# Last layer's edge pass: both ends' parts meet with channels on partitions, destination rows become TensorE weights, scan resets spread by a product

## Chip, core and metric

The kernel runs on one core of a Trainium2 chip. The metric is the device time of one execution in microseconds. A core has five engines that run side by side and meet at semaphores: PE (matmul; PEld is its weight load), DVE (elementwise, scans), ACT (activation functions), POOL and SP. SP here only issues DMAs. SBUF is the on-chip memory, PSUM the banks that PE writes.

## What is computed

Four graph layers over 6250 nodes of 128 channels and 106250 edges, sorted by destination; between them a layer norm with the residual. The change touches only the last one:

```python
f_src = (feat @ W_src.T + b_src).reshape(n, HEADS, OUT_FEATS)
f_dst = (feat @ W_dst.T + b_dst).reshape(n, HEADS, OUT_FEATS)
f_v = (feat @ W_v.T + b_v).reshape(n, HEADS, OUT_FEATS)
a = f_src[src] + f_dst[dst]
e = jnp.where(a >= 0, a, NEG_SLOPE * a)
sa = _edge_softmax(e, dst, n)          # per channel, over the edges of a destination
m = f_v[src] * sa
rst = jax.ops.segment_sum(m, dst, num_segments=n)
```

The softmax is per channel: for each destination and channel the maximum over its edges, the exponentials of what lies below it, their sum.

## The kernel before

Each layer is a pass over the edges (`edges0` to `edges3`) and a pass over the nodes (`after0` to `after3`). An edge pass goes over items: an item is a chunk of 128 edges together with a tile of 128 nodes that holds their destinations. Four items are a group, and there are 220 groups. `pipeline` runs the groups in steps: in step v every stage with lag k works on group v - k, and within a step each engine takes its stages in the order of the list that `ps.run` gets. That list is the whole schedule; a step is as long as its slowest ring of waits. Ten steps are one turn of a hardware loop.

In `edges3`, for one group:

- `gather` (lag 0): SP waits for `s_others` and `s_gap` of two groups ago, then loads `near` (L926; two buffers), a row of 516 floats spread to all 128 partitions, which says for each edge which node of the tile it belongs to. POOL gathers the rows of the edges' sources (L808, four indirect DMAs), 256 floats an edge: the source part and the value part. Every fifth step SP also loads indices (L792).
- `load_resets` (lag 2): SP waits for the backward scan of two groups before (`s_top`), then spreads a row of `reset_d` to all partitions (L1359): 0 within a destination, hugely negative where the next one begins.
- `turn` (lag 0, ACT): L1371 and L1377 make the selector `sel_t` (node on partitions, edge along the row) out of `near`; `not_first` (L1384) and `from_first` (L1391, gap) follow. `s_gap` releases the next load of `near`.
- `both_ends` (lag 1, PE): `sel_t` as weights times the nodes' destination parts (L1400, `side(...)` is the destination part of a tile in `acc`, its place read from a register), plus a product with `ident` that adds the source parts (L1402). The result has edges on partitions.
- `take` (lag 2, ACT L1406) copies it, `leaky` (lag 2, DVE L1411) applies the slope. `by_channel` (lag 2, PE L1419) transposes, so that channels are on partitions.
- `forward` (lag 3, DVE L1430): a scan along the edges, state = max(state + reset, logit), in place in PSUM. `backward` (lag 3, DVE L1438): the same from the right. Now each edge holds its destination's maximum, in `top`.
- `below_top` (lag 4, PE): `top` times -1 (L1484) brings the maximum back to edges on partitions, a product with `ident` adds the logit (L1486). `exps` (lag 4, ACT L1490).
- `message` (lag 5): exponentials times values, L1496, items 0 and 1 on POOL, 2 and 3 on DVE. `sums_a` and `sums_b` (lag 5, PE L869) multiply with the selector `sel` (made by ACT, L844 and L852) and so add up per node; DVE adds four items to `acc` (lag 6, L893) behind a rescaling (L1475).

PE's order in a step is `below_top`, `both_ends`, `by_channel`, `factors`, `sums_a`, `sums_b`; DVE's is `leaky`, `scaled`, three adds, `message`, the last add, `forward`, `backward`; SP's is near, indices, resets.

Of the kernel before, what the change touches and what calls it, by code (L numbers as in the profile page):

```python
# [15 lines left out]
P = 128  # L16
N_NODES = 6250
N_EDGES = 106250
D = 128
# [22 lines left out]
LOW = -3.0e38  # L42
# [108 lines left out]
def build(nc, a):  # L151
    PE, V, A, G, SP = nc.tensor, nc.vector, nc.scalar, nc.gpsimd, nc.sync
# [3 lines left out]
    def dram(name, shape, dt=F32):  # L156
        return nc.dram_tensor(name, shape, dt).ap()
# [3 lines left out]
    reset_d = dram("reset_d", [ITEMS_PAD // GROUP, GROUP * P])  # L161
# [17 lines left out]
    def sb(ctx, name, shape, dt=F32):  # L179
        return ctx.enter_context(nc.sbuf_tensor(name, shape, dt))  # L180
# [12 lines left out]
    ident = sb(root, "ident", [P, P])  # L193
# [21 lines left out]
    def tables(ctx, closing, loaded_x, loaded_qkv, made_ident, cleared_x):  # L215
# [102 lines left out]
        m = pe.did(m)  # L318
# [38 lines left out]
        reset = sb(ctx, "reset", [P, ITEM_TILES, P])  # L357
# [582 lines left out]
    def quad(b, width=P):  # L940

        return bank[b][:, 0:GROUP * width].rearrange("p (i d) -> p i d", i=GROUP)
# [376 lines left out]
    def edges3():  # L1319
# [3 lines left out]

        with Phase(nc, "e3") as ctx:
            ps = EdgePass(ctx, fsv_t, 2 * D, W3, sels=2, turns=1)
            EDGES = GROUP * P
            resets = ps.sb("resets", [P, 2, EDGES + 1])
# [7 lines left out]
            s_resets = [ps.sem(f"resets{u}") for u in range(2)]  # L1335
            s_a, s_taken, s_l, s_turned, s_run, s_top, s_d, s_exp, s_msg_g, s_msg_v = (
                ps.sem(n) for n in ("a", "taken", "l", "turned", "run", "top", "d", "exp", "msg_g", "msg_v"))
# [6 lines left out]
            V.memset(resets[:, :, EDGES:], 0.0).then_inc(start, 1)  # L1344
# [48 lines left out]
            def both_ends(g):  # L1393
                tiles = ps.tiles(g, PE_ENGINE)
                ps.have_rows(PE, g)
                PE.wait_ge(by_node.s_t, g.upto(0))
                if g.old(2):
                    PE.wait_ge(s_l, g.upto(-2))
                for i in range(GROUP):
                    PE.matmul(bank[B_A[g.r2]][:, i * P:(i + 1) * P], by_node.sel_t[:, g.r2, i, :],  # L1400
                              side(ds(tiles[i], 1)).rearrange("p a d -> p (a d)"), start=(i == 0), stop=False)
                PE.matmul(quad(B_A[g.r2]), ident[:], ps.row(g)[:, :, 0:D], start=False, stop=True).then_inc(s_a, 1)  # L1402

            def take(g):
                A.wait_ge(s_a, g.upto(0))
                A.activation(ps.row(g)[:, :, 0:D], quad(B_A[g.r2]), ACT.Copy).then_inc(s_taken, 1)  # L1406

            def leaky(g):

                V.wait_ge(s_taken, g.upto(0))  # L1410
                V.scalar_tensor_tensor(out=ps.row(g)[:, :, 0:D], in0=quad(B_A[g.r2]), scalar=0.2,  # L1411
                                       in1=ps.row(g)[:, :, 0:D], op0=ALU.mult, op1=ALU.max).then_inc(s_l, 1)
# [12 lines left out]
            def forward(g):  # L1425
                V.wait_ge(s_turned, g.upto(0))
                V.wait_ge(s_resets[g.r2], (g.turn(2) + 1) * 16)
                if g.old(1):
                    V.wait_ge(s_top, g.upto(-1))
                V.tensor_tensor_scan(bank[B_L[g.r2]], resets[:, g.r2, 0:EDGES], bank[B_L[g.r2]],  # L1430
                                     top_before(g), ALU.add, ALU.max).then_inc(s_run, 1)

            def backward(g):
                V.wait_ge(s_run, g.upto(0))
                if g.old(SPAN):
                    V.wait_ge(s_d, g.upto(-SPAN))
                    V.wait_ge(s_rise, g.upto(1 - SPAN))
                V.tensor_tensor_scan(top[:, g.at(SPAN), ::-1], resets[:, g.r2, EDGES:0:-1],  # L1438
                                     bank[B_L[g.r2]][:, ::-1], LOW, ALU.add, ALU.max).then_inc(s_top, 1)
# [39 lines left out]
            def below_top(g):  # L1479
                PE.wait_ge(s_top, g.upto(0))  # L1480
                if g.old(1):
                    PE.wait_ge(s_exp, g.upto(-1))
                for i in range(GROUP):
                    PE.matmul(bank[B_D][:, i * P:(i + 1) * P], top[:, g.at(SPAN), i * P:(i + 1) * P], minus[:],  # L1484
                              start=(i == 0), stop=False)
                PE.matmul(quad(B_D), ident[:], ps.row(g)[:, :, 0:D], start=False, stop=True).then_inc(s_d, 1)  # L1486

            def exps(g):
                A.wait_ge(s_d, g.upto(0))
                A.activation(ps.row(g)[:, :, 0:D], quad(B_D), ACT.Exp).then_inc(s_exp, 1)  # L1490

            def message(engine, s_msg, items):
                def stage(g):
                    engine.wait_ge(s_exp, g.upto(0))
                    values = ps.row(g)[:, items, D:2 * D]
                    engine.tensor_tensor(values, values, ps.row(g)[:, items, 0:D], ALU.mult).then_inc(s_msg, 1)  # L1496
                return stage

            def sums_a(g):
                PE.wait_ge(s_msg_g, g.upto(0))  # L1500
                PE.wait_ge(ps.s_sel, g.upto(0))
                ps.scatter(g, lambda i: [(0, ps.row(g)[:, i, :])], (0, 1))

            def sums_b(g):
                PE.wait_ge(s_msg_v, g.upto(0))
                ps.scatter(g, lambda i: [(0, ps.row(g)[:, i, :])], (2, 3))

            ps.run([(0, gather), (2, load_resets), (5, message(G, s_msg_g, slice(0, 2))),
                    (4, below_top), (1, both_ends), (2, by_channel), (5, factors), (5, sums_a), (5, sums_b),
# [3 lines left out]
                    (5, message(V, s_msg_v, slice(2, 4))), (6, ps.add(3)), (3, forward), (3, backward)])  # L1513
# [59 lines left out]
```

## Time and profile before

| | |
|---|---|
| median of 3 runs | 5292.35 us (5288.9 to 5292.99) |
| profiled execution | 5294.54 us, span 5292.8 us |
| busy over the whole span | PE 3755.0 us (71%), DVE 3648.3 (69%), ACT 2912.2 (55%), POOL 3691.8 (70%) |
| last layer's edge pass | about 3848 to 5190 us of the span |
| SP's DMAs in it | near 258.0 KB, resets 256.0 KB a group; indices 10.0 KB every fifth |

Busy time is the time in which an engine has an instruction; for PE the ends are modelled, and instructions overlap. PEclk is the clock that PE was granted, as a share of 2.4 GHz; its other level is 1.2 GHz (0.50). The DMA share is the mean busy share of the core's 16 DMA engines. In the last edge pass the pattern repeats every 6 us or so, so one step on the time line and one table over many steps tell nearly everything. In rows with "issue" as releaser, the engine waited for nothing that the profile shows.

### The profile page before, as it was taken

To read this page: it belongs to the slowest core of one execution; us is meant where nothing else is said; L and a number is where in the kernel's file an instruction comes from. 1 tells how busy PE (TensorE), PEld (TensorE's weight loads), DVE (VectorE), ACT (ScalarE), POOL (GpSimd) and SP (SyncE) were. 2 spreads that over 40 slices of the span, in tenths; PEclk is the share of its full clock that TensorE was granted. 3 is DMA by queue.
4 is the path that set the end of the run, shared out by engine and by line. 5 is a ranking of instruction groups with operands and counts; after the bars stand their busy time and mean duration, and the time that the engine had idled before them with its cause. 6 is when DMAs were issued, how large, how long until landed. Compare 5 with 4: busy or idle time off the path is not lost. (4 is left out here: it accounts for less than half of the span.)

```text
span 5292.8 us, 95054 instructions
## 1 busy us (share of the span) xinstructions
PE 3755.0 (71%) x19843; PEld 3029.5 (57%) x19844; DVE 3648.3 (69%) x8656; ACT 2912.2 (55%) x7558; POOL 3691.8 (70%) x3835
## 2 busy tenths in 40 slices
PE   5444544441666566666678888888779999999992
PEld 4444444441555555555466666666657777777771
DVE  5666666667644444445577777777668989989997
ACT  2444444443522222223566666666469989999993
POOL 4777777773777777774377777777067777777772
PEclk8777877875777777777688898998989999999996
DMA  7444444442433333331111111111156666666661
GB/s 193 143 155 159 153 151 152 152 152 75 114 79 77 76 78 78 79 78 42 48 55 56 55 55 55 55 56 55 51 155 177 177 174 176 176 177 176 176 178 39
DMA packets 394829, 596.70 MB, mean 113 GB/s; under 512 B 115000, under 2 KB 224718, under 8 KB 394352
## 3 DMA queue, kind: packets, MB, share of 16 engines
q0 software_dynamic: 141696, 349.47, 23.6%
q1 hardware_dynamic: 252176, 245.81, 15.8%
q8 instruction: 32, 0.52, 0.0%
q10 hardware_dynamic: 864, 0.39, 0.0%
q14 instruction: 61, 0.50, 0.0%
HBM read 563.33 MB, written 30.30 MB: 112 GB/s over the span
## 5 line engine op out<-in xcount | busy, mean ns | idle before, releaser
L893 DVE TENSOR_TENSOR acc<-acc,banks 128x256 f32 (+1 forms) x3520 | 1360.8, 387 | 756.5 <-PE banks L869 486.2
L808 POOL DMA_INDIRECT e_rows<-kv_t,e_index x800 | 786.6, 983 | 243.7 <-issue 240.9
L808 POOL DMA_INDIRECT e_rows<-x_t,e_index x800 | 781.0, 976 | 248.6 <-issue 243.2
L808 POOL DMA_INDIRECT e_rows<-up_t,e_index x800 | 774.9, 969 | 243.8 <-issue 238.3
L808 POOL DMA_INDIRECT e_rows<-fsv_t,e_index x800 | 779.1, 974 | 227.0 <-issue 211.2
L869 PE MATMUL banks<-e_rows,e_sel 128*128 128x256 f32 x3520 | 904.1, 403 | 6.3 <-ACT e_rows L1095 3.8
L844 ACT ACTIVATE e_away<-node_iota,local 128x128 f32<-128x128 f32 x2640 | 840.5, 389 | 8.4 <-issue 0.9
L869 PE MATMUL banks<-e_msg,e_sel 128*128 128x137 f32 (+1 forms) x3520 | 760.8, 365 | 9.9 <-DVE acc L893 4.5
L869 PEld LDWEIGHTS banks<-e_rows,e_sel 128*128 128x128 f32 x3520 | 681.7, 204 | 99.3 <-issue 6.8
L970 PE MATMUL banks<-acc,e_sel_t 128*128 x1760 | 312.3, 333 | 586.2 <-DVE e_sel_t L937 571.8
L1095 ACT ACTIVATE e_rows<-banks,e_rows 128x128 f32<-128x128 f32 x880 | 250.7, 370 | 799.5 <-PE banks L1086 384.1
L869 PEld LDWEIGHTS banks<-e_msg,e_sel 128*128 128x128 f32 x3520 | 625.5, 219 | 60.5 <-DVE acc L893 4.9
L970 PEld LDWEIGHTS banks<-acc,e_sel_t 128*128 128x128 f32 x1760 | 272.0, 236 | 621.8 <-issue 620.9
L1086 PE MATMUL banks<-e_w,e_attr 65*128 65x128 f32 x1760 | 289.3, 317 | 406.4 <-DMA e_attr<-in_attr_rows 406.0
L1086 PEld LDWEIGHTS banks<-e_w,e_attr 65*128 65x128 f32 x1760 | 275.6, 228 | 439.9 <-issue 387.0
L852 ACT ACTIVATE e_sel<-e_away,ones_col 128x512 f32<-128x512 f32 x660 | 473.4, 717 | 21.3
L999 ACT ACTIVATE e_msg<-e_clip 128x32 f32<-128x32 f32 x220 | 51.1, 232 | 658.6 <-DVE e_clip L995 657.6
L937 DVE TENSOR_SCALAR e_sel_t<-e_near,node_step 128x512 f32<-128x512 f32 x220 | 113.1, 514 | 319.0 <-DMA e_near<-near_d 318.9
L1400 PEld LDWEIGHTS banks<-acc,e_sel_t 128*128 128x128 f32 x1760 | 232.5, 193 | 129.2 <-issue 129.2
L1221 PE MATMUL banks<-e_emb,e_w 16*128 16x256 f32 x440 | 164.7, 456 | 180.9 <-DMA e_emb<-emb_d 161.4
L1430 DVE TENSOR_TENSOR_SCAN banks<-e_resets,e_top,banks 128x512 f32<-128x512 f32 x220 | 281.9, 1282 | 0.0
L1438 DVE TENSOR_TENSOR_SCAN e_top<-e_resets,banks 128x512 f32<-128x512 f32 x220 | 268.6, 1221 | 10.8 <-DVE banks L1430 3.9
(202 smaller groups left out, 6973.4 us busy)
## 6 DMA issues: line engine op xcount, KB each, us to landing
e_near<-near_d SPq DMA_DIRECT2D x440, 258.0 KB, 5.2
e_resets<-reset_d SPq DMA_DIRECT2D x220, 256.0 KB
e_attr<-in_attr_rows SPq DMA_DIRECT2D x880, 32.0 KB
e_rows<-kv_t,e_index POOLq DMA_INDIRECT x800
e_rows<-x_t,e_index POOLq DMA_INDIRECT x800
e_rows<-up_t,e_index POOLq DMA_INDIRECT x800
e_rows<-fsv_t,e_index POOLq DMA_INDIRECT x800
kv_t<-proj_kv SPq DMA_DIRECT2D x12, 512.0 KB, 5.3
```

The lines of the kernel that those rows point to most:

```text
L808: G.indirect_dma_start(out=self.rows[:, u, i, 0:self.width], out_offset=None, in_=self.table, in_offset=bass.IndirectOffsetOnAxis(ap=index ...
L844: m = A.activation(away[:, i, :], node_iota[:], ACT.Abs, bias=local[:, ds(g.n * GROUP + i, 1)], scale=-1.0)
L852: A.activation(self.place_of_sel(g), away[:], ACT.Relu, bias=ones_col[:], scale=-1.0).then_inc(self.s_sel, 1)
L869: m = PE.matmul(bank[n_bank][:, col + at:col + at + rows.shape[1]], self.place_of_sel(g)[:, i, :], rows, start=True, stop=True)
L893: V.tensor_tensor(to, to, bank[n_bank][:, col:col + self.sums].unsqueeze(1), ALU.add).then_inc(self.s_added[i], 1)
L970: m = PE.matmul(bank[B_Q[g.r2]][:, i * P:(i + 1) * P], by_node.sel_t[:, g.r2, i, :], side(ds(tiles[i], 1)).rearrange("p a d -> p (a d)"), ...
L1086: m = PE.matmul(bank[B_H[g.r2]][:, i * P:(i + 1) * P], attr[:, g.at(SPAN), i, :], w1[:], start=True, stop=True)
L1095: m = A.activation(ps.row(g)[:, i, D + 1:], bank[B_H[g.r2]][:, i * P:(i + 1) * P], ACT.Relu, scale=ps.row(g)[:, i, 0:1])
L1221: PE.matmul(hidden_bank(g, 0), w0[:], emb[:, g.at(SPAN), :], start=True, stop=True).then_inc(s_h1, 1)
L1400: PE.matmul(bank[B_A[g.r2]][:, i * P:(i + 1) * P], by_node.sel_t[:, g.r2, i, :], side(ds(tiles[i], 1)).rearrange("p a d -> p (a d)"), star ...
L1430: V.tensor_tensor_scan(bank[B_L[g.r2]], resets[:, g.r2, 0:EDGES], bank[B_L[g.r2]], top_before(g), ALU.add, ALU.max).then_inc(s_run, 1)
L1438: V.tensor_tensor_scan(top[:, g.at(SPAN), ::-1], resets[:, g.r2, EDGES:0:-1], bank[B_L[g.r2]][:, ::-1], LOW, ALU.add, ALU.max).then_inc(s_ ...
```

## The change

Both parts of the logit now meet with channels on partitions. `both_ends` transposes the gathered source parts into the bank and adds a product whose weights are the destination parts of the tile and whose moving side is `sel_t`. The weights are no longer read from `acc` under a register; SP copies each of the group's four tiles into a buffer `far` first (`load_far`). `take` and `leaky` write `logit`, five groups deep, and `by_channel` goes. The resets are loaded as one BF16 row, and PE spreads them to the 128 partitions of a PSUM bank by a product with a row of ones (`spread_resets`, lag 3). The scans read the resets there; the forward scan writes `top` in SBUF, the backward one runs in place over its 511 other elements. `below_top` transposes the logits back and adds the negated tops, with two banks instead of one. POOL multiplies one item of the message instead of two, DVE three. `load_resets` moves from lag 2 to lag 1 and waits for `s_r` of two groups before.

```diff
-            resets = ps.sb("resets", [P, 2, EDGES + 1])
+            far = ps.sb("far", [P, 2, GROUP, P])
+            logit = ps.sb("logit", [P, SPAN, EDGES])
+            resets = ps.sb("resets", [1, 2, EDGES], BF16)
+            ones_row = ps.sb("ones_row", [1, P], BF16)
...
-            B_A, B_L, B_D, B_F = (2, 3), (4, 5), 6, 7
+            B_A, B_D, B_R, B_F = (2, 3), (4, 5), 6, 7
...
+            def load_far(g):
+
+                tiles = ps.tiles(g, SP_ENGINE)
+                if g.old(2):
+                    SP.wait_ge(s_a, g.upto(-2))
+                for i in range(GROUP):
+                    SP.dma_start(far[:, g.r2, i, :], side(ds(tiles[i], 1)).rearrange("p a d -> p (a d)")
+                                 ).then_inc(s_far[g.r2], 16)
+
             def load_resets(g):
                 if g.old(2):
-                    SP.wait_ge(s_top, g.upto(-2))
-                SP.dma_start(resets[:, g.r2, 0:EDGES], reset_d[ds(g.n, 1), :].to_broadcast([P, EDGES])
-                             ).then_inc(s_resets[g.r2], 16)
+                    SP.wait_ge(s_r, g.upto(-2))
+                SP.dma_start(resets[:, g.r2, :], reset_d[ds(g.n, 1), :]).then_inc(s_resets[g.r2], 16)
...
             def both_ends(g):
-                tiles = ps.tiles(g, PE_ENGINE)
                 ps.have_rows(PE, g)
                 PE.wait_ge(by_node.s_t, g.upto(0))
+                PE.wait_ge(s_far[g.r2], (g.turn(2) + 1) * 64)
                 if g.old(2):
                     PE.wait_ge(s_l, g.upto(-2))
                 for i in range(GROUP):
-                    PE.matmul(bank[B_A[g.r2]][:, i * P:(i + 1) * P], by_node.sel_t[:, g.r2, i, :],
-                              side(ds(tiles[i], 1)).rearrange("p a d -> p (a d)"), start=(i == 0), stop=False)
-                PE.matmul(quad(B_A[g.r2]), ident[:], ps.row(g)[:, :, 0:D], start=False, stop=True).then_inc(s_a, 1)
+                    PE.matmul(bank[B_A[g.r2]][:, i * P:(i + 1) * P], ps.row(g)[:, i, 0:D], ident[:],
+                              start=(i == 0), stop=False, is_transpose=True)
+                for i in range(GROUP):
+                    m = PE.matmul(bank[B_A[g.r2]][:, i * P:(i + 1) * P], far[:, g.r2, i, :],
+                                  by_node.sel_t[:, g.r2, i, :], start=False, stop=(i == GROUP - 1))
+                m.then_inc(s_a, 1)
...
-            def by_channel(g):
-                PE.wait_ge(s_l, g.upto(0))
-                if g.old(2):
-                    PE.wait_ge(s_top, g.upto(-2))
-                for i in range(GROUP):
-                    m = PE.transpose(bank[B_L[g.r2]][:, i * P:(i + 1) * P], ps.row(g)[:, i, 0:D], ident[:])
-                m.then_inc(s_turned, 1)
+            def spread_resets(g):
+                PE.wait_ge(s_resets[g.r2], (g.turn(2) + 1) * 16)
+                if g.old(1):
+                    PE.wait_ge(s_top, g.upto(-1))
+                PE.matmul(bank[B_R], ones_row[:], resets[:, g.r2, :], start=True, stop=True).then_inc(s_r, 1)
...
-                V.tensor_tensor_scan(bank[B_L[g.r2]], resets[:, g.r2, 0:EDGES], bank[B_L[g.r2]],
-                                     top_before(g), ALU.add, ALU.max).then_inc(s_run, 1)
...
+                V.tensor_tensor_scan(top[:, g.at(SPAN), :], bank[B_R], logit[:, g.at(SPAN), :],
+                                     top_before(g), ALU.add, ALU.max).then_inc(s_run, 1)
+
+            def backward(g):
+
+                V.wait_ge(s_run, g.upto(0))
+                back = top[:, g.at(SPAN), EDGES - 2::-1]
+                V.tensor_tensor_scan(back, bank[B_R][:, EDGES - 1:0:-1], back, top[:, g.at(SPAN), EDGES - 1:EDGES],
+                                     ALU.add, ALU.max).then_inc(s_top, 1)
...
                 for i in range(GROUP):
-                    PE.matmul(bank[B_D][:, i * P:(i + 1) * P], top[:, g.at(SPAN), i * P:(i + 1) * P], minus[:],
-                              start=(i == 0), stop=False)
-                PE.matmul(quad(B_D), ident[:], ps.row(g)[:, :, 0:D], start=False, stop=True).then_inc(s_d, 1)
+                    PE.matmul(bank[B_D[g.r2]][:, i * P:(i + 1) * P], logit[:, g.at(SPAN), i * P:(i + 1) * P], ident[:],
+                              start=(i == 0), stop=False, is_transpose=True)
+                for i in range(GROUP):
+                    m = PE.matmul(bank[B_D[g.r2]][:, i * P:(i + 1) * P], top[:, g.at(SPAN), i * P:(i + 1) * P], minus[:],
+                                  start=False, stop=(i == GROUP - 1))
+                m.then_inc(s_d, 1)
...
-            ps.run([(0, gather), (2, load_resets), (5, message(G, s_msg_g, slice(0, 2))),
-                    (4, below_top), (1, both_ends), (2, by_channel), (5, factors), (5, sums_a), (5, sums_b),
+            ps.run([(0, gather), (0, load_far), (1, load_resets), (5, message(G, s_msg_g, slice(0, 1))),
+                    (4, below_top), (3, spread_resets), (1, both_ends), (5, factors), (5, sums_a), (5, sums_b),
...
-                    (5, message(V, s_msg_v, slice(2, 4))), (6, ps.add(3)), (3, forward), (3, backward)])
+                    (5, message(V, s_msg_v, slice(1, 4))), (6, ps.add(3)), (3, forward), (3, backward)])
```

## Rows read from the trace of the kernel before

**Rows 1.** Windows, all engines: busy us (instructions) by engine, PEclk, DMA share, GB/s

```profile
2904.60:2908.00 3.40, 0.10 (x1) 0.11 (x2) 1.90 (x6) 0.56 (x1) 2.49 (x4) 1.00 0.20 51
...
866.00:877.00 11.00, 6.29 (x48) 5.69 (x48) 9.45 (x27) 6.74 (x20) 8.56 (x9) 1.00 0.35 105
4200.00:4800.00 600.00, 594.65 (x3311) 450.38 (x3310) 541.28 (x905) 546.99 (x1405) 463.80 (x502) 1.00 0.63 176
```

**Rows 2.** Waits from 4200 to 4800: us in total, times, longest

```profile
ACT e_apart L1371 <- DMA e_near<-near_d: 38.7, 82, 1.7
PEld banks L1484 <- DVE e_top L1438: 26.3, 84, 0.9
...
DVE e_rows L1411 <- ACT e_rows L1406: 5.8, 14, 1.2
```

**Rows 3.** Time line of SP and ACT from 4507: start, length in us

```profile
4507.06 0.33 SPq L926 DMA_DIRECT2D e_near<-near_d  x1
4510.65 0.72 ACT L1371 ACTIVATE e_apart<-e_near,e_minus_node 128x512 f32<-128x512 f32 x1 [0.35 <-DMA e_near<-near_d]
...
4512.36 0.39 ACT L1391 ACTIVATE e_gap<-node_iota,e_near 128x128 f32<-128x128 f32 x1
4512.97 0.34 SPq L926 DMA_DIRECT2D e_near<-near_d  x1
4513.54 0.51 SPq L792 DMA_DIRECT2D e_index<-src  x1
4516.38 0.72 ACT L1371 ACTIVATE e_apart<-e_near,e_minus_node 128x512 f32<-128x512 f32 x1
```

**Rows 4.** Line L926 from 4200 to 4800: duration, first and last start

```profile
L926 SPq DMA_DIRECT2D e_near<-near_d x101: 332/333/338, 4200.7 to 4799.2; - x101
```

**Rows 5.** Time line of DVE, a step in which it isn't kept waiting

```profile
4221.68 0.67 DVE L1411 SCALAR_TENSOR_TENSOR e_rows<-banks,e_rows 128x512 f32<-128x512 f32 x1
...
4224.38 0.42 DVE L1496 TENSOR_TENSOR e_rows<-e_rows 128x256 f32<-128x256 f32 x1
4224.72 0.41 DVE L893 TENSOR_TENSOR acc<-acc,banks 128x256 f32 x1
4225.05 1.28 DVE L1430 TENSOR_TENSOR_SCAN banks<-e_resets,e_top,banks 128x512 f32<-128x512 f32 x1
4226.36 1.22 DVE L1438 TENSOR_TENSOR_SCAN e_top<-e_resets,banks 128x512 f32<-128x512 f32 x1
4227.50 0.67 DVE L1411 SCALAR_TENSOR_TENSOR e_rows<-banks,e_rows 128x512 f32<-128x512 f32 x1
```

**Rows 6.** Time line of PE, a step from its beginning

```profile
4503.81 1.09 PE L1484 MATMUL banks<-e_minus,e_top 128*128 128x128 f32 x8
4504.74 1.02 PE L1486 MATMUL banks<-e_rows,ident 128*128 128x512 f32 x2
4505.60 1.05 PE L1400 MATMUL banks<-acc,e_sel_t 128*128 x8
4506.49 1.02 PE L1402 MATMUL banks<-e_rows,ident 128*128 128x512 f32 x2
4507.35 0.60 PE L1419 MATMUL banks<-ident,e_rows 128*128 128x128 f32 x4
4507.79 0.27 PE L1464 MATMUL banks<-ident,e_at_first 128*128 128x128 f32 x1
```

**Rows 7.** Groups of DVE instructions, first layer's pass, 500 to 1100: busy, mean ns

```profile
L1004 DVE TENSOR_TENSOR e_msg<-e_rows,e_msg 128x512 f32<-128x512 f32 x118 | 80.9, 685 | 0.0
```

**Rows 8.** Time line of SP in the second layer's pass: DMAs of 32 KB with dynamic addresses

```profile
1699.70 6.55 SPq L1078 DMA_DIRECT2D e_attr<-in_attr_rows  x9
```

**Rows 9.** SP's own waits from 4200 to 4800

```profile
SPq L1359 <- DVE e_top L1438: 250.0, 100, 3.1
```

**Rows 10.** DMA queue of SP, 4200 to 4800 and 5225 to 5290: packets, MB, share of 16 engines

```profile
q1 hardware_dynamic: 31762, 52.99, 30.9%
...
q1 hardware_dynamic: 6444, 3.20, 17.1%
```

More of the change, by code:

```diff
@@ L160, in build @@
     item_rows = dram("item_rows", [2, ITEMS_PAD], I32)
-    reset_d = dram("reset_d", [ITEMS_PAD // GROUP, GROUP * P])
+    reset_d = dram("reset_d", [ITEMS_PAD // GROUP, GROUP * P], BF16)
     rhat_d = dram("rhat_d", [P, ITEMS_PAD, 3])
@@ L356, in tables @@
         near = sb(ctx, "near", [P, ITEM_TILES, P + 1])
-        reset = sb(ctx, "reset", [P, ITEM_TILES, P])
+        reset = sb(ctx, "reset", [P, ITEM_TILES, P], BF16)
         yield V, 2.2
@@ L1334, in edges3 @@
             apart = ps.sb("apart", [P, GROUP, P])
-            s_resets = [ps.sem(f"resets{u}") for u in range(2)]
-            s_a, s_taken, s_l, s_turned, s_run, s_top, s_d, s_exp, s_msg_g, s_msg_v = (
-                ps.sem(n) for n in ("a", "taken", "l", "turned", "run", "top", "d", "exp", "msg_g", "msg_v"))
+            s_resets, s_far = ([ps.sem(f"{n}{u}") for u in range(2)] for n in ("resets", "far"))
+            s_a, s_taken, s_l, s_r, s_run, s_top, s_d, s_exp, s_msg_g, s_msg_v = (
+                ps.sem(n) for n in ("a", "taken", "l", "r", "run", "top", "d", "exp", "msg_g", "msg_v"))
             s_apart, s_gap, s_rise, s_shrink, s_first, s_f, s_others, s_scaled, start = (
                 ps.sem(n) for n in ("apart", "gap", "rise", "shrink", "first", "f", "others", "scaled", "start"))
-            B_A, B_L, B_D, B_F = (2, 3), (4, 5), 6, 7
+            B_A, B_D, B_R, B_F = (2, 3), (4, 5), 6, 7
             by_node = ByNode(ps, s_a, 2)
@@ L1343, in edges3 @@
             V.memset(top[:, SPAN - 1, :], LOW).then_inc(start, 1)
-            V.memset(resets[:, :, EDGES:], 0.0).then_inc(start, 1)
+            V.memset(ones_row[:], 1.0).then_inc(start, 1)
             V.tensor_scalar(minus[:], ident[:], -1.0, None, ALU.mult).then_inc(start, 1)
@@ L1399, in both_ends @@
                 for i in range(GROUP):
[L1400 to L1402 removed]
+                    PE.matmul(bank[B_A[g.r2]][:, i * P:(i + 1) * P], ps.row(g)[:, i, 0:D], ident[:],
[4 more added lines that the diff above has]
+                m.then_inc(s_a, 1)
             def take(g):
                 A.wait_ge(s_a, g.upto(0))
[L1406 removed]
+                if g.old(SPAN):
+                    A.wait_ge(s_d, g.upto(-SPAN))
+                A.activation(logit[:, g.at(SPAN), :], bank[B_A[g.r2]], ACT.Copy).then_inc(s_taken, 1)
             def leaky(g):
                 V.wait_ge(s_taken, g.upto(0))
[L1411 to L1420 removed]
+                V.scalar_tensor_tensor(out=logit[:, g.at(SPAN), :], in0=bank[B_A[g.r2]], scalar=0.2,
+                                       in1=logit[:, g.at(SPAN), :], op0=ALU.mult, op1=ALU.max).then_inc(s_l, 1)
+            def spread_resets(g):
[3 more added lines that the diff above has]
+                PE.matmul(bank[B_R], ones_row[:], resets[:, g.r2, :], start=True, stop=True).then_inc(s_r, 1)
             def top_before(g):
@@ L1425, in forward @@
             def forward(g):
-                V.wait_ge(s_turned, g.upto(0))
-                V.wait_ge(s_resets[g.r2], (g.turn(2) + 1) * 16)
+                V.wait_ge(s_l, g.upto(0))
+                V.wait_ge(s_r, g.upto(0))
                 if g.old(1):
                     V.wait_ge(s_top, g.upto(-1))
-                V.tensor_tensor_scan(bank[B_L[g.r2]], resets[:, g.r2, 0:EDGES], bank[B_L[g.r2]],
+                if g.old(SPAN):
+                    V.wait_ge(s_d, g.upto(-SPAN))
+                    V.wait_ge(s_rise, g.upto(1 - SPAN))
+                V.tensor_tensor_scan(top[:, g.at(SPAN), :], bank[B_R], logit[:, g.at(SPAN), :],
                                      top_before(g), ALU.add, ALU.max).then_inc(s_run, 1)
```

15 lines of the change are left out of this document (5 added, 10 removed).

## Prediction

> **What bounds the kernel now.** I read the page first: nothing outside the last layer's edge pass is touched, so only its 220 steps count (a step is one group of four items). There PE looks like the bound: in 600 us of steady running it is busy for 594.65, at the full clock, against 541 for DVE, 547 for ACT and 464 for POOL [rows 1]. The change takes work off PE, so the question is whether that busy figure is a bound. A busy figure with modelled ends can't say; the waits can, and then the time line.
>
> The list of waits says that PE waits for DVE (PEld L1484 on the backward scan, 84 times in 101 steps, 26.3 us), DVE waits for ACT's copy 14 times (5.8 us), and ACT waits for the DMA of near 82 times (38.7 us of 600, the largest wait that isn't "issue" among those that end at another engine or a DMA) [rows 2]. So the chain of blame ends at a DMA, and the reader should see what that DMA itself waits for. On the time line near is issued at 4507.06, ACT's L1371 starts on it at 4510.65, L1391 starts at 4512.36 and lasts 0.39, and 0.22 later, at 4512.97, the next near goes out [rows 3]. That is a closed ring, because near has two buffers: load(g) waits for gap(g-2), which ACT makes one step before it needs near(g). Its length in this step is 3.59 (issue to start) + 1.71 + 0.39 + 0.22 = 5.91 us. Over the stretch 101 issues lie between 4200.7 and 4799.2, which is 598.5 / 100 = 5.985 us a step [rows 4]. With 2.32 us for the three fixed terms, the mean from issue to use is 5.985 - 2.32 = 3.66 us. The ring accounts for the whole step, and there is no PE in it.
>
> Two other chains lie just under it. DVE's step, where it isn't kept waiting, is 4227.50 - 4221.68 = 5.82 us [rows 5]. PE's step is 5.985 less the 0.26 us that PEld waits for the backward scan, about 5.7 [rows 2]. POOL and ACT have more room; ACT waits 0.4 us a step.
>
> **The change part by part.** My sum is made against the profiled execution, 5294.54 us with a span of 5292.8; the median of the runs is 5292.35, so 2.2 us are taken off at the end.
>
> *PE.* Removed: the two 512-column products with ident, 0.86 each (4504.74 to 4505.60, 4506.49 to 4507.35), and the by_channel transposes, 0.44 (4507.35 to 4507.79). Added: two sets of four transposes at 0.44 and the spread of the resets. The far products keep L1400's 0.89, the top products L1484's 0.93 [rows 6]. The spread is one pass over 512 columns in BF16; no row shows it. From below it is a single 128-column transpose, 0.11, from above a 512-column product in F32, 0.86; I take a quarter of that, 0.22, since L1402 takes two records for its 0.86 and each column of a transpose costs half of those again. Sum: -0.86 -0.86 -0.44 +0.88 +0.22 = -1.06 us a step, 233 us over 220 steps. I cost this saving at nothing: PE would stand idle for about 1.3 us instead of 0.3. Its step still begins at DVE's backward scan, and its sums still need ACT's selector of the same step.
>
> *DVE.* leaky keeps shape and operand kinds (PSUM and SBUF in, SBUF out). The forward scan now writes SBUF instead of PSUM. Backward already does, and takes 1.22 against 1.28 [rows 5]; so -0.06, bounds -0.06 and 0 (both scans now read the resets from PSUM and the data from SBUF, one PSUM operand as before; +0.06 each is the far end if the operand's place matters). The message goes from two items to three. 512 elements out of SBUF take 0.685 [rows 7], 256 take 0.42, so 128 more cost 0.133. Sum +0.07: DVE's floor becomes 5.82 + 0.07 = 5.89 us, bounds 5.82 and 6.01. This is the price that matters: whatever else the change frees, a step can't fall by more than 5.985 - 5.89 = 0.095 us, or 21 us in all.
>
> *POOL.* Its message loses one of two items. It isn't on the ring, so nothing is gained.
>
> *ACT.* The same instructions with the same shapes; take writes logit instead of rows. Zero. Two new waits (take on s_d of five steps ago) are long fulfilled.
>
> *SP and the DMA queues.* This is where the ring can be hurt. Per step the 256 KB broadcast of the resets goes, a row of 1 KB comes, and four SBUF-to-SBUF copies of 64 KB come with a register load, directly behind near. In the second layer's pass nine such DMAs with a dynamic address, with their register loads, take 6.55 us, 0.73 each [rows 8]; four are 2.9 us of SP. SP has them in the step's 5.985 us beside near, the resets and every fifth step the indices. What stands behind them is load_resets, which now waits for PE's spread instead of for DVE's backward scan: 1.37 + 0.22 + about 0.2 later than that scan's end. PE's step of 4503.81 [rows 6] has its successor near 4509.8, so the spread is done at about 4511.6, SP is through with the resets half a us later, 4512.1, and gap ends at 4512.75. So near isn't held up as long as DVE is no more than 0.6 us late. SP's present waits, 2.5 us a step for the scan, say that there is room [rows 9]. Price 0; if the cover is gone, each us of lateness goes into the ring in full.
>
> The load on the DMA engines: near and resets are 30.9% of the 16 engines, about 15.5% each. The 512-byte packets of the output (6444 of them, 17.1% of 16 engines over 65 us) cost 0.0276 us each [rows 10]; 512 of them a step are 14.1 us on 16 engines, 14.8% of 5.985. So far weighs what the resets weighed. It only moves: resets went out some 3 us before near, far goes out up to 3 us behind it. Near's landing of 3.66 us is the term that decides, and no row shows it with four DMAs behind. The nearest is 4512.97, with the index DMA 0.57 behind it: 3.41 to L1371, against 3.59 for the one before without [rows 3]. Bounds: 0.15 shorter (no resets ahead, gathers less backed up) and 0.3 longer (near shares the engines with its followers); ACT's longest single wait, 1.7 us, shows that landings do stretch. I take 0 for the mean.
>
> The Trainium skill speaks against the far copies: DMA: Bandwidth & Descriptors (Bandwidth) asks for DMAs of 1 MiB and gives 0.95 us for one of 64 KB. An estimate by that page would be 3.8 us of DMA time a step for the four (measured there for DMAs that another engine issues), against 0.88 by the packets of this trace. What it would mean here is rival 5.
>
> **Sum.** The ring stays at 5.985. It has some scatter, which DVE today makes good between long landings; with DVE's floor raised that costs a little, and with the resets gone from ahead of near a little comes back. I put the net at -0.02 us a step: 220 x -0.02 = -4 us, 5290.3 on the profiled execution and 5288 against the median.
>
> **Rivals.**
> 1. *The followers delay near.* For it: one queue, four DMAs behind it in every step, gathers in between. Against it: near's packets are first in their queue and the engines' load is equal. 0.1 to 0.3 us a step, 22 to 66 us; middle 5325. It decides from a landing of 3.72 on, since there is no slack in the ring: 0.05 x 220 = 11 us. This is the case slower than before.
> 2. *PE is the bound after all*, or the landing gets shorter by 0.1 or more. Both end at the same wall, DVE's 5.89: -0.095 x 220 = -21, 5272. For it: 99% busy, and the broadcast ahead of near is gone. Against it: the ring closes without PE, and PE waits for DVE in most steps.
> 3. *DVE's new floor binds.* If the scans dislike the resets in PSUM (+0.06 each), the floor is 6.01 and the step with it: +0.03 x 220, 5298; with ordinary lateness on top, 5303.
> 4. *PE's clock.* PE gets idle time. In this trace the clock stays at 2.4 GHz with PE only 57% busy in 866 to 877, and falls to 1.2 GHz behind the stretch from 2904.6, in which it did 0.1 us of work in 3.4 [rows 1]. With 1.3 us idle in 6 I expect the first. If it fell in one step of five, the 1.6 us from the scan's end to the spread would double there, use up the 0.6 of slack and delay near by 1.0: 0.2 a step, +44, 5332. By TensorE: Matmul & The Clock Gate (Part 1: The HAM clock gate) of the Trainium skill the throttled clock is the default and activity lifts it, so that less work is a risk; the row at 57% speaks against it here.
> 5. *Small transfers are dear.* If a far packet cost what one of the resets does (15.5% for 128), 512 would be 62%, the DMA load 0.63 - 0.155 + 0.62 = 1.10 and the step 5.985 x 1.10 = 6.56: +127, 5415. The output's packets speak against it. It is how the page above would come true.
> 6. *The change doesn't do what it says*: the old copies and products stay. The diff removes them; under 1%.
>
> **How the numbers follow.** Forecast (landing within -0.09 and +0.05 of now) 44%, 5280 to 5300. Rival 1 20%, rival 2 25%, rival 3 5%, rival 4 with other lateness of SP 4%, rivals 5 and 6 2%. Two runs of this kernel can be told apart from about 0.2%, 10.6 us. Of the forecast a few hundredths fall beyond either edge; faster 0.28, same 0.44, slower 0.28. The range goes from 5270, just under DVE's wall, to 5330, which takes in most of rival 1; about 2 in 10 stay outside.
>
> **What would show it.** In the changed kernel's trace: step time by the issues of near; issue of near to L1371's successor (3.66 now); ACT's wait for near (0.4 us a step now; gone if DVE's wall is reached); DVE's unhindered step, 5.89; scans at 1.22 both; the message on DVE at 0.55; PE about 1.3 us idle a step, its clock at 1.00; DMA share still near 0.63. I am wrong if near's landing moves by more than 0.1 us, if SP issues near later than 0.22 us behind gap, or if DVE's step isn't 5.89.

## The result, and the profile after

The changed kernel takes 5305.98 us (median of 8 runs, 5301.47 to 5308.46), the kernel before 5289.11 us (8 runs, 5285.12 to 5295.06) on the same chip. The ratio is 1.003, with a 95% interval from 1.0019 to 1.004: slower by 17 us. The profiled execution has a span of 5306.7 us. The predicted 5288 lay on the other side of no change; the time is inside the range of 5270 to 5330.

The loss lies in the last layer's pass. In the two profiled executions, whose spans are 5292.8 and 5306.7 us, the time from the first to the last issue of near grows by 16.2 us; this pass starts 2.0 us earlier, and the part behind the last near changes by 0.3. A step of the pass is read from the issues of near over a long stretch, 4000 to 5100 us (columns: instructions; shortest, median and longest ns; first and last start). Before:

```profile
L926 SPq DMA_DIRECT2D e_near<-near_d x184: 332/333/338, 4005.0 to 5098.1; - x184
```

and after:

```profile
L926 SPq DMA_DIRECT2D e_near<-near_d x182: 332/349/353, 4003.6 to 5099.0; - x182
```

That is 1093.1 / 183 = 5.973 us a step before and 1095.4 / 181 = 6.052 after. The difference, 0.079 us, times 220 steps is 17.4 us, as much as the medians differ by: the loss is in the length of the step.

The windows row of after, 4200 to 4800 us (busy us and instructions of PE, PEld, DVE, ACT, POOL; PEclk; DMA share; GB/s), stands against the last line of [rows 1]:

```profile
4200.00:4800.00 600.00, 530.40 (x3374) 427.99 (x3375) 549.35 (x894) 540.65 (x1388) 430.23 (x497) 1.00 0.63 174
```

PE lost 64 us of 595, the clock stayed at 2.4 GHz (1.00), and the DMA share is the 0.63 of before. The only engine that is busier is DVE, though it did fewer steps. The waits of after in the same stretch say where PE's gain went, and what became of the ring (us in total, times, longest):

```profile
PEld banks L1503 <- DVE e_top L1457: 84.0, 85, 1.3
PE banks L1503 <- DVE e_top L1457: 57.4, 91, 0.9
ACT e_apart L1386 <- DMA e_near<-near_d: 47.1, 95, 1.1
...
DVE e_logit L1430 <- ACT e_logit L1426: 0.4, 2, 0.2
...
SPq L1375 <- PE banks L1437: 138.2, 97, 2.0
SPq L925 <- ACT e_gap L1406: 14.3, 37, 1.0
```

PE's saving became waiting for DVE's backward scan: the wait of PE's weight loads is 84.0 us instead of 26.3 [rows 2]. ACT still waits for near, and a bit longer. The lines that decide are DVE's and the last one: DVE waits for ACT only twice, 0.4 us (before 14 times, 5.8 us [rows 2]), and SP holds near back for gap in only 37 of 99 steps. In the kernel before it did so in every one:

```profile
SPq L925 <- ACT e_gap L1391: 225.0, 101, 3.5
```

So the ring of near, closed in each step before, is mostly open after: the near for the next step is free to go when SP gets to it. What is closed instead is DVE's own chain. Its time line in after, from one forward scan to the next (start, length, both us):

```profile
4299.89 1.27 DVE L1450 TENSOR_TENSOR_SCAN e_top<-banks,e_top,e_logit 128x512 f32<-128x512 f32 x1
4301.19 1.28 DVE L1457 TENSOR_TENSOR_SCAN e_top<-banks,e_top 128x511 f32<-128x511 f32 x1
4302.39 0.66 DVE L1430 SCALAR_TENSOR_TENSOR e_logit<-banks,e_logit 128x512 f32<-128x512 f32 x1
4302.98 0.47 DVE L1494 SCALAR_TENSOR_TENSOR acc<-banks,e_others,acc 128x256 f32 x1
4303.55 0.98 DVE L893 TENSOR_TENSOR acc<-acc,banks 128x256 f32 x2
4304.75 0.42 DVE L893 TENSOR_TENSOR acc<-acc,banks 128x256 f32 x1 [0.21 <-DVE acc L893]
4305.09 0.55 DVE L1519 TENSOR_TENSOR e_rows<-e_rows 128x384 f32<-128x384 f32 x1
4305.55 0.41 DVE L893 TENSOR_TENSOR acc<-acc,banks 128x256 f32 x1
4305.89 1.27 DVE L1450 TENSOR_TENSOR_SCAN e_top<-banks,e_top,e_logit 128x512 f32<-128x512 f32 x1
...
4311.89 1.27 DVE L1450 TENSOR_TENSOR_SCAN e_top<-banks,e_top,e_logit 128x512 f32<-128x512 f32 x1
...
4317.89 1.27 DVE L1450 TENSOR_TENSOR_SCAN e_top<-banks,e_top,e_logit 128x512 f32<-128x512 f32 x1
```

The scan starts at 4299.89, 4305.89, 4311.89 and 4317.89: a step of exactly 6.00 us, again and again, with no wait for another engine. So regular a beat points to the engine that bounds; in the kernel before, whose ring goes through a DMA, the step varies more (the forward scan starts at 4242.49, 4248.60, 4254.41 and 4260.32: 6.11, 5.81 and 5.91 us). The difference is one of degree. Between 4000 and 5100 us, 144 of 182 steps of after lie within 0.03 us of the shortest; in the kernel before it is 86 of 184. So the kernel before, too, runs nearly half of its steps at DVE's own 5.82 us; the others are longer. In after some longer steps (such as 4347.90 to 4354.51) lift the mean to 6.05.

DVE's unhindered step was 5.82 [rows 5]; the prediction had 5.89 for after, and it is 6.00. Two lines of each kernel, from the groups of instructions of 4200 to 4800 (busy us, mean ns), hold most of the answer. Before:

```profile
L1430 DVE TENSOR_TENSOR_SCAN banks<-e_resets,e_top,banks 128x512 f32<-128x512 f32 x101 | 129.4, 1282 | 0.0
L1438 DVE TENSOR_TENSOR_SCAN e_top<-e_resets,banks 128x512 f32<-128x512 f32 x100 | 122.1, 1221 | 5.0 <-DVE banks L1430 1.9
```

After:

```profile
L1457 DVE TENSOR_TENSOR_SCAN e_top<-banks,e_top 128x511 f32<-128x511 f32 x100 | 128.0, 1280 | 3.5
L1450 DVE TENSOR_TENSOR_SCAN e_top<-banks,e_top,e_logit 128x512 f32<-128x512 f32 x99 | 126.2, 1275 | 0.0
...
L1519 DVE TENSOR_TENSOR e_rows<-e_rows 128x384 f32<-128x384 f32 x99 | 55.1, 556 | 0.0
```

The forward scan didn't get shorter (1.282 to 1.275), and the backward scan, costed at no change, got longer by 0.059 us. With the message's 0.134 that is 5.82 - 0.007 + 0.059 + 0.134 = 6.006.

### The profile page after: what moved, and what is told of

The parts are those of the page before. It is cut to its first block and busy times, and to the rows that moved or that the text cites. A ratio compares the mean times of both kernels' runs of the same rounds, so it can differ in the third digit from the quotient of the medians.

```text
span 5306.7 us, 96549 instructions
## 1 busy us (share of the span) xinstructions
PE 3639.6 (69%) x20063; PEld 3004.1 (57%) x20064; DVE 3680.0 (69%) x8656; ACT 2909.3 (55%) x7558; POOL 3627.0 (68%) x3835
## 5 line engine op out<-in xcount | busy, mean ns | idle before, releaser
L869 PE MATMUL banks<-e_rows,e_sel 128*128 128x256 f32 x3520 | 920.6, 408 | 22.9 <-issue 14.7
L970 PEld LDWEIGHTS banks<-acc,e_sel_t 128*128 128x128 f32 x1760 | 274.0, 237 | 617.4 <-issue 616.5
L1457 DVE TENSOR_TENSOR_SCAN e_top<-banks,e_top 128x511 f32<-128x511 f32 x220 | 281.7, 1280 | 7.8
L1450 DVE TENSOR_TENSOR_SCAN e_top<-banks,e_top,e_logit 128x512 f32<-128x512 f32 x220 | 280.5, 1275 | 0.3 <-issue 0.3
L1252 PEld LDWEIGHTS banks<-e_w,e_h 65*128 65x128 f32 x1760 | 259.6, 212 | 18.2 <-issue 3.8
```

Source lines behind the costliest of these rows:

```text
L869: m = PE.matmul(bank[n_bank][:, col + at:col + at + rows.shape[1]], self.place_of_sel(g)[:, i, :], rows, start=True, stop=True)
L970: m = PE.matmul(bank[B_Q[g.r2]][:, i * P:(i + 1) * P], by_node.sel_t[:, g.r2, i, :], side(ds(tiles[i], 1)).rearrange("p a d -> p (a d)"), ...
L1252: m = PE.matmul(bank[B_W[g.r2]][:, i * P:(i + 1) * P], h2[:, g.r2, i * P:(i + 1) * P], w2[:], start=True, stop=True)
L1450: V.tensor_tensor_scan(top[:, g.at(SPAN), :], bank[B_R], logit[:, g.at(SPAN), :], top_before(g), ALU.add, ALU.max).then_inc(s_run, 1)
L1457: V.tensor_tensor_scan(back, bank[B_R][:, EDGES - 1:0:-1], back, top[:, g.at(SPAN), EDGES - 1:EDGES], ALU.add, ALU.max).then_inc(s_top, 1)
```

## The experiments

Theory A: DVE's chain of 6.00 us binds, and is longer than the 5.82 of before by the third message item (0.13) and the backward scan (0.06). Rivals: near is held up behind SP's new order or by the far copies (rival 1 of the prediction); the resets in PSUM make the scans dear (the mechanism of rival 3). A chip's own median differs a little from the next one's, so each comparison below is with runs of the kernel before on the same chip. Steps are worked out as above, from the issues of near between 4000 and 5100 us.

**The message back at two items and two, in the changed kernel.**

```
-message(G, s_msg_g, slice(0, 1))    message(V, s_msg_v, slice(1, 4))
+message(G, s_msg_g, slice(0, 2))    message(V, s_msg_v, slice(2, 4))
```

(and the sums take items 0 and 1, then 2 and 3).

> The changed kernel with the message split as before: items 0 and 1 on POOL, 2 and 3 on DVE. Theory A (DVE's own chain of 6.00 us sets the changed kernel's step, since the message takes 0.134 us more and the scans read a PSUM operand): the chain falls to 5.87 us, the ring of near (2.32 + 3.59 = 5.91 us, and what SP adds) binds next, the step goes from 6.05 to about 5.95 us, the time from 5306 to about 5284 us. Theory B (SP's new work sets the step: four copies, and the wait for the spread ahead of near): DVE's part doesn't matter, 5306 us within 4.

5316.08 us against 5312.17 (ratio 1.0008, 0.9999 to 1.0017). The changed kernel itself was not run on this chip; against its ratios of 1.003 and 1.0034 on two others, most of the loss is gone. But the gain on the kernel before that theory A had expected isn't there. DVE's shortest steps fell to 5.87 us (4257.88 to 4263.75), and near's ring closed again: SP waited for gap in 89 of 99 steps. The expectation had taken near's landing from the first chip. Here the step is (5097.5 - 4002.2) / 180 = 6.085 us, and the time from the issue of near to the start of ACT's L1386 on it, taken for each near of the trace, has a mean of 3.72 us, against 3.62 in the kernel before on the first chip.

```profile
SPq L925 <- ACT e_gap L1406: 47.3, 89, 1.0
```

**The message at one item and three, in the kernel before**: the same edit the other way round.

> The kernel before with the message split of the changed one: item 0 on POOL, 1 to 3 on DVE, nothing else. Theory A: DVE's chain goes from 5.82 to 5.95 us, just under the ring's 5.97, so that DVE can't make good long landings any more: step 6.00 to 6.03 us, time 5289 + 220 x 0.04 = 5298 us (5295 to 5302). Theory B: nothing on SP changed, 5289 us.

```profile
4202.95 1.28 DVE L1430 TENSOR_TENSOR_SCAN banks<-e_resets,e_top,banks 128x512 f32<-128x512 f32 x1
...
4208.90 1.28 DVE L1430 TENSOR_TENSOR_SCAN banks<-e_resets,e_top,banks 128x512 f32<-128x512 f32 x1
```

5322.06 us (ratio 1.002, 1.001 to 1.0029): about 10 us slower, as theory A had it. DVE's shortest step is now 5.95 us. The third item on DVE (POOL has one less) costs time by itself, with none of the rest of the change there. It does so although the ring is closed in this kernel (SP waits for gap in 99 of 99 steps). That fits with the steps at DVE's own length counted above: with a longer one, DVE makes good less after a late landing. No run shows this reason by itself.

**Near with five buffers, in the kernel before.** This opens the ring and changes nothing else.

```
-by_node = ByNode(ps, s_a, 2)        g.old(2): SP.wait_ge(s_others, g.upto(-2))
+by_node = ByNode(ps, s_a, 5)        g.old(5): SP.wait_ge(s_others, g.upto(-5))
-by_node.near[:, g.r2, ...]          # in first() and turn()
+by_node.near[:, g.at(5), ...]
```

> The kernel before with five buffers for near instead of two, so that its load may go out three steps earlier. If the ring of near sets the step before (issue to use 3.66 us + 2.32 us of ACT and SP), it opens: ACT's wait for near (0.40 us a step) goes, the step falls to DVE's chain of 5.82 us with its loop end, about 5.87, and the time to 5289 - 220 x 0.11 = 5265 us. If PE or DVE set it already, 5289 us within 4.

5254.81 us against 5312.17 (ratio 0.9893, 0.9878 to 0.9908), 57 us faster (4 runs): the fastest kernel of this study. The expectation, made from the first chip, was 24 us. The step is (5095.2 - 4004.1) / 187 = 5.835 us; against the 5.973 of the kernel before on the first chip that would be 30 us, an estimate. The landings are longer on this chip, so there is more to win; there is no trace of the kernel before on it that would show its step. SP has no wait for gap left, and DVE's forward scans start at a beat of 5.82 us:

```profile
4298.35 1.28 DVE L1430 TENSOR_TENSOR_SCAN banks<-e_resets,e_top,banks 128x512 f32<-128x512 f32 x1
...
4304.17 1.28 DVE L1430 TENSOR_TENSOR_SCAN banks<-e_resets,e_top,banks 128x512 f32<-128x512 f32 x1
...
4309.98 1.28 DVE L1430 TENSOR_TENSOR_SCAN banks<-e_resets,e_top,banks 128x512 f32<-128x512 f32 x1
```

while the windows row has PE busy all the time:

```profile
4200.00:4800.00 600.00, 600.00 (x3396) 461.29 (x3394) 547.52 (x927) 564.81 (x1439) 472.21 (x515) 1.00 0.60 180
```

This confirms the reading of the kernel before: near's ring bound it and PE, at 594.65 of 600 [rows 1], did not; PE has done 2% more steps in the same 600 us without any of its work removed. That DVE is next, and not PE with its 600.00, is read from the waits: PE's weight loads wait for the backward scan 92 times in 4200 to 4800 us, and DVE waits 1.4 us in all for another engine (ACT). The change makes just that engine's step longer. The changed kernel with five buffers was not run, so what the change would be worth with the ring open is not shown.

**The resets broadcast into SBUF in BF16, in the changed kernel**, without the product that spreads them into PSUM. `load_resets` is back at lag 2 and waits for the backward scan, as in the kernel before.

```
-SP.dma_start(resets[:, g.r2, :], reset_d[ds(g.n, 1), :])                  # [1, 2, EDGES]
+SP.dma_start(resets[:, g.r2, :], reset_d[...].to_broadcast([P, EDGES]))   # [P, 2, EDGES]
-V.tensor_tensor_scan(top[...], bank[B_R], logit[...], ...)
+V.tensor_tensor_scan(top[...], resets[:, g.r2, :], logit[...], ...)
```

> The changed kernel with the resets spread by the DMA into SBUF again (in BF16, 128 KB a group), no product for them; the scans have no operand in PSUM. Theory A: both scans lose the PSUM read, 1.28 to 1.22 us each, DVE's chain falls from 6.00 to 5.88 us, the step to about 5.96 us, the time to 5306 - 220 x 0.09 = 5286 us. If the 0.06 us is not the operand's place (but, say, the reversed or in-place access), the scans stay at 1.28 and the time at 5306. Theory B (near held up by SP's wait for the spread): that wait goes too, 5290 us or less, but with the scans' length unchanged or not, ACT's wait for near falls.

```profile
L1455 DVE TENSOR_TENSOR_SCAN e_top<-e_resets,e_top 128x511 f32<-128x511 bf16 x96 | 123.6, 1288 | 3.4
L1448 DVE TENSOR_TENSOR_SCAN e_top<-e_resets,e_top,e_logit 128x512 f32<-128x512 bf16 x96 | 122.6, 1278 | 0.0
...
4200.00:4800.00 600.00, 489.30 (x3138) 409.06 (x3139) 536.63 (x857) 518.53 (x1332) 492.01 (x476) 0.99 0.71 188
```

5355.49 us (ratio 1.0079, 1.0065 to 1.0092). No operand of either scan is in PSUM, and they still take 1.28 us: the mechanism of rival 3 falls. (The resets are BF16 here, a second difference; in `before_ptr` below they are F32 in SBUF and the scans take 1.28 us as well.) The run is slower for another reason. The broadcast of 128 KB in every step raises the DMA share to 0.71, and the step is (5096.9 - 4004.6) / 173 = 6.314 us. SP waits for gap in 94 of 95 steps, so the ring binds, and 6.31 less the fixed 2.32 leaves 3.99 us from issue to use. The kernel before with the message at one and three, on the same chip, has a share of 0.63 and (5097.9 - 4002.4) / 180 - 2.32 = 3.77 us. Taken near by near from the traces the means are 3.96 and 3.74. So near lands later where more is moved beside it; how much of that is the load and how much the order in SP's queue, this run doesn't tell apart. Theory A's 5286 us did not come, since the scans did not get shorter and the load was not in its sum. Within this change, the spread by a product was the cheaper way: 1.0079 here against 1.003 and 1.0034 for the changed kernel on other chips.

What was left as a difference between the one scan that took 1.22 us and the rest was the initial value: the backward scan of the kernel before has an immediate (LOW), and all the others read theirs from a tile. Theory P is that this makes the 0.06 us; theory Q, that it is something about the operands or working in place. Four kernels ran on one chip for it (kernel before: 5299.28 us, 27 runs), the first of them the changed kernel itself.

> The changed kernel itself, as the reference of this call: both theories expect 1.003 of the kernel before, with a step of 6.05 us between 4200 and 4800 us, backward scan 1.280 us and message 0.47 us from start to start.

5318.33 us, ratio 1.0034 (1.0021 to 1.0048), step 6.080, scans 1.274 and 1.281 us.

**The backward scan with an immediate, in the changed kernel.**

```
-V.tensor_tensor_scan(back, ..., back, top[:, g.at(SPAN), EDGES - 1:EDGES], ALU.add, ALU.max)
+V.tensor_tensor_scan(back, ..., back, LOW, ALU.add, ALU.max)
```

> The changed kernel with the backward scan's initial value as the immediate LOW instead of a pointer to the last edge of forward's result; this leaves out what the last edge hands back, so its maxima are not the reference's. Theory P (a scan whose initial value is read through a pointer takes 0.06 us longer than one with an immediate): the backward scan falls from 1.280 to 1.22 us, VectorE's shortest step from 6.00 to 5.94 us; if VectorE's chain is what binds now, the step falls by up to 0.06 us, 220 x 0.06 = 13 us, ratio 1.0005 to 1.0015 instead of 1.003, less where near's ring takes over. Theory Q (the time of the scan comes from its operands or from working in place): the scan stays at 1.28 us and the ratio at 1.003.

```profile
L1457 DVE TENSOR_TENSOR_SCAN e_top<-banks,e_top 128x511 f32<-128x511 f32 x100 | 122.1, 1221 | 3.4
...
4366.51 1.28 DVE L1450 TENSOR_TENSOR_SCAN e_top<-banks,e_top,e_logit 128x512 f32<-128x512 f32 x1
...
4372.45 1.28 DVE L1450 TENSOR_TENSOR_SCAN e_top<-banks,e_top,e_logit 128x512 f32<-128x512 f32 x1
```

This leaves out what the last edge's maximum hands back to the edges before it. The tensors it works on, the lengths and working in place are the same; the scan falls to 1.221 us and DVE's shortest step to 5.94. 5307.50 us, ratio 1.0014 (1.0005 to 1.0023), 10.8 us less than the changed kernel.

**The same, and the message at two and two.** Both price rises of DVE are taken back, everything else of the change stays.

> The same, and the messages shared 2 and 2 as in the kernel before; both price rises of VectorE are taken back. Theory P: VectorE's shortest step 5.81 to 5.82 us as before; near's ring binds, as it does in the kernel before, so the time is that of the kernel before, ratio 0.9985 to 1.001. If something else of the change cost time (the later issue of near, the wait for the product), the ratio stays above 1.002 though VectorE's chain is as short as before.

5302.30 us, ratio 1.0004 (0.9995 to 1.0013). DVE's shortest steps are those of the kernel before,

```profile
4341.71 1.28 DVE L1450 TENSOR_TENSOR_SCAN e_top<-banks,e_top,e_logit 128x512 f32<-128x512 f32 x1
...
4347.52 1.27 DVE L1450 TENSOR_TENSOR_SCAN e_top<-banks,e_top,e_logit 128x512 f32<-128x512 f32 x1
```

5.81 us, and the ring is what remains (SP waits for gap in 83 of 100 steps). Of the 19 us by which the changed kernel is slower on this chip, 16.0 are DVE's two terms; the other 3 are within the interval of no change. So the rest of the change, the far copies, the later resets and the spread against what it takes off PE, comes to nothing that can be measured; only this sum is shown, not each part of it.

**The backward scan with a pointer, in the kernel before.** A column of LOW in place of the immediate.

```
+low = ps.sb("low", [P, 1])          V.memset(low[:], LOW)
-V.tensor_tensor_scan(top[:, g.at(SPAN), ::-1], ..., bank[B_L[g.r2]][:, ::-1], LOW, ...)
+V.tensor_tensor_scan(top[:, g.at(SPAN), ::-1], ..., bank[B_L[g.r2]][:, ::-1], low[:], ...)
```

> The kernel before with the backward scan's initial value LOW read through a pointer to a column of 128 values instead of an immediate; nothing else changes and the result is the same. Theory P: the backward scan rises from 1.221 to 1.28 us, VectorE's shortest step from 5.82 to 5.88 us; near's ring binds at 5.97 us, so only a part shows, ratio 1.000 to 1.0015. Theory Q: the scan stays at 1.221 us, ratio 1.000.

```profile
L1440 DVE TENSOR_TENSOR_SCAN e_top<-e_resets,e_low,banks 128x512 f32<-128x512 f32 x100 | 128.0, 1280 | 5.1 <-DVE banks L1432 1.9
...
4309.93 1.28 DVE L1432 TENSOR_TENSOR_SCAN banks<-e_resets,e_top,banks 128x512 f32<-128x512 f32 x1
...
4315.81 1.28 DVE L1432 TENSOR_TENSOR_SCAN banks<-e_resets,e_top,banks 128x512 f32<-128x512 f32 x1
```

1.221 becomes 1.280 us by the initial value alone, and the shortest step 5.82 becomes 5.88. Theory P stands, theory Q falls. The time is 5303.35 us (ratio 1.0007, 0.9998 to 1.0016), which can't be told from no change; 220 times 0.06 would be 13 us.

Put side by side, the runs with two buffers for near go up with DVE's shortest step, in either kernel (each ratio against the kernel before on its own chip):

| run | DVE's shortest step, us | ratio |
|---|---|---|
| after_low_msg22 | 5.81 | 1.0004 |
| after_msg22 | 5.87 | 1.0008 |
| before_ptr | 5.88 | 1.0007 |
| after_low | 5.94 | 1.0014 |
| before_msg13 | 5.95 | 1.002 |
| the changed kernel, two chips | 6.00 | 1.003, 1.0034 |

**Gap made in the step of its near**, one step earlier, on both kernels, to see what near's issue is worth. These four ran on a chip on which every kernel takes some 6590 us and the engines stand waiting on "issue" and on unrelated transfers for microseconds at a time, so that a step of this pass is 7.3 to 7.5 us; they settle nothing about this change, and neither theory is judged by them. None of the gains expected of them came.

```
-(0, not_first), (1, from_first), (5, at_firsts),
+(0, not_first), (5, at_firsts), (0, from_first),
```

> The changed kernel with from_first moved from lag 1 to lag 0, behind at_firsts in ACT's order, so that near's buffer comes free one step earlier; no instruction more or less. Theory A: the ring opens, and what is left is DVE's chain of 6.00 us with its loop end (6.04 us a step): 220 x 0.01 to 220 x 0.07 under the unaltered changed kernel, 2 to 15 us, by how long the landings of this chip are. Theory B: near still waits for SP's four copies and the spread, no change or slower.

The changed kernel itself had a ratio of 1.0007 there (0.9985 to 1.0029), with the earlier gap 1.0035 (1.0016 to 1.0054), the latter with messages at two and two 1.0044 (1.0023 to 1.0064), and the kernel before with the earlier gap 1.0004 (0.9982 to 1.0027). Whether an earlier gap opens the ring without more buffers is left open.

## Why the prediction was wrong

- **What bounds the kernel before**: right. Five buffers for near took 57 us off, with PE's work untouched.
- ***PE***: right that the saving is worth nothing. It is idle time in after, 57.4 of PE's 69.6 us of it in waits for the backward scan. The saving itself was mis-sized: from the first product of a step to the `factors` transpose PE takes 4305.72 - 4302.53 = 3.19 us, where it took 4507.79 - 4503.81 = 3.98 [rows 6], so 0.79 less and not 1.06, and it is idle for 0.7 us a step and not 1.3. The spread takes 4304.33 - 4304.01 = 0.32 us, not 0.22, four transposes 0.49 and not 0.44; PE's idle time hides it all (PE's time line of after):

```profile
4302.53 0.66 PE L1503 MATMUL banks<-ident,e_logit 128*128 128x128 f32 x4 [0.66 <-DVE e_top L1457]
4303.02 1.06 PE L1506 MATMUL banks<-e_minus,e_top 128*128 128x128 f32 x8
4304.01 0.39 PE L1437 MATMUL banks<-e_resets,e_ones_row 1*128 1x512 bf16 x1
4304.33 0.66 PE L1415 MATMUL banks<-ident,e_rows 128*128 128x128 f32 x4
4304.82 1.06 PE L1418 MATMUL banks<-e_sel_t,e_far 128*128 128x128 f32 x8
4305.72 0.27 PE L1483 MATMUL banks<-ident,e_at_first 128*128 128x128 f32 x1
```

- ***DVE***, the scans: this is the step that failed. The prediction read 1.28 against 1.22 as the price of writing PSUM, and took 0.06 off forward. The two rows differ in more than the place of the result: in direction, and in the initial value, which the instruction's name even shows (e_top among the inputs of L1430, nothing such in L1438 [rows 5]). The change leaves forward's pointer and gives backward one. So forward stayed (-0.007 instead of -0.06) and backward rose (+0.059 instead of 0): 0.11 us of floor that the sum lacked. The prediction had the right size as a bound, +0.06 for each scan, by a wrong mechanism and with 5% on it; that its 6.01 meets the measured 6.00 is luck.
- ***DVE***, the message: +0.134 against 0.133 forecast.
- **The sum** went from a floor of 5.89, under the ring's 5.985, to one of 6.00, over it. The wall that was to stop a gain became the bound. The step of 6.05 is that floor and some lateness; rival 3 had a floor of 6.01 and 5303 us with lateness. A second term was too small as well: a raised floor still under the ring was to cost "a little", for a net of -0.02 us a step. A floor of 5.95 under a closed ring cost about 10 us in `before_msg13`, 0.045 a step, and with floors of 5.87 and 5.88, near the forecast's own 5.89, the runs are at 1.0008 and 1.0007, neither clear of no change. No run with two buffers shows a gain over the kernel before, so nothing shows that a floor of 5.89 would have brought the forecast gain of 4 us. (5294.54 less 220 x 0.02 is 5290.1, not 5290.3; the 5288 stands.)
- ***SP and the DMA queues***: right in the sum. The DMA share is 0.63 as before, and SP's queue takes 31.8% of the engines instead of 30.9% [rows 10]:

```profile
q1 hardware_dynamic: 74632, 52.58, 31.8%
```

  Its 512-byte packets, which are the far copies, take 27.1 ns each in 4200 to 4800 us and 14.4% of the engines, where the output's rows had given 27.6 and 14.8%. Rival 5 is out, and with it the estimate by DMA: Bandwidth & Descriptors (Bandwidth) of the Trainium skill; the trace differs from it: four copies of 64 KB a step left the load where it was. Rival 1 is out too: in the time line of after, near goes out at 4305.16 and L1386 starts on it at 4308.61, 3.45 us, which lies between the 3.41 and 3.59 of [rows 3]; over all nears between 4000 and 5100 us the mean is 3.59 us after and 3.62 before. (Rival 1's 5325 isn't the middle of its own 22 to 66 us: that is 44 us, and 5288 + 44 = 5332.) The slack of 0.6 us on SP was too hopeful, though: near goes out 0.34 us behind gap's end in the mean, 0.22 before. In the step that follows the spread (4310.01, 0.39 long) holds the resets until 4310.69, and near leaves 0.52 us behind gap's end at 4310.72, not 0.22 (SP and ACT of after):

```profile
4305.16 0.35 SPq L926 DMA_DIRECT2D e_near<-near_d  x1
...
4310.69 0.28 SPq L1375 DMA_DIRECT2D e_resets<-reset_d  x1
4311.24 0.33 SPq L926 DMA_DIRECT2D e_near<-near_d  x1
...
4308.61 0.72 ACT L1386 ACTIVATE e_apart<-e_near,e_minus_node 128x512 f32<-128x512 f32 x1 [0.22 <-DMA e_near<-near_d]
...
4310.33 0.39 ACT L1406 ACTIVATE e_gap<-node_iota,e_near 128x128 f32<-128x128 f32 x1
```

  With DVE's terms taken back, the same order on SP and the rest of the change together cost nothing that can be measured.
- ***PE's clock***: right, 1.00 in 4200 to 4800 us with PE busy for 530.40 of 600. Rival 4 is out.

## What to carry to other kernels

Where two chains are within 3% of each other, as here, count on both: the change left the first alone, added 0.19 us to the second and lost time, and the work that it took off a third engine, 99% busy, showed no gain. When two rows of one instruction differ in time, list everything in which they differ, the scalar operands too, before a price is hung on one of it; and ask of each edit which of those properties it moves. First open the ring (here, three more buffers, -57 us), then see which engine's step is next, and only then move work between engines.

## What the runs showed of the hardware

- A tensor_tensor_scan over 512 F32 columns takes 1.221 us with an immediate as initial value and 1.280 with one read from a column of a tile: shown in both directions, by one edit each on either kernel. With operands and result in PSUM or in SBUF, and with F32 or BF16 resets, the rows with a column lie between 1.274 and 1.288 us.
- The load of near, itself untouched, came 0.22 us later with 128 KB a step more beside it: at a DMA share of 0.71 instead of 0.63, issue to use was 3.99 us instead of 3.77. The order in SP's queue differed too. From chip to chip, it differed by about 0.1 us.
- A 512-byte packet of the copies inside SBUF took 27.1 ns of a DMA engine in this pass, a 2064-byte packet of near 123.4 ns.
- A PE busy figure of 600.00 us in 600 did not mean that PE bounds: with near's ring open DVE kept a beat of 5.82 us and waited for no other engine but for 1.4 us, and with 594.65 us of 600 PE had still room for 2% more steps.
